# A two-layer attention and mixture block: the layer-0 mixing spread over three engines, with reordered stages

## The reference

```python
xn = _layernorm(x)
x = x + attention0(xn) + ffn0(xn)
# ffn0: x_norm = rms(xn); logits = x_norm @ W.T + base
#   H_res = sinkhorn(H_res_logits / 0.1, 50 iterations); H_res = (1 - g) * I + g * H_res
#   H_pre, H_post = softmax(...), softmax(...)
#   y = einsum('btnc,btn->btc', streams, H_pre) @ W_branch
#   out = einsum('btij,btjc->btic', H_res, streams) + einsum('btc,btn->btnc', y, H_post)
xn = _layernorm(x)
x = x + attention1(xn) + ffn1(xn)
# attention1: q = xn @ Wq.T; latent k, v = down, then up; 32 heads, 4 of them on one key head, causal
# ffn1: xf @ weight.T + sum over the top 2 of 8 experts of gate * (xf @ A) @ B / 16
```

## Time and profile before

| | us |
|---|---|
| median of 3 runs (2345.44 to 2351.66) | 2350.42 |
| the profiled execution: time | 2352.82 |
| its span, granted TensorE clock 0.984 | 2351.0 |
| stage B begins; first sum of its scaling; its last reciprocal; last operation | 85.8; 86.8; 192.1; 238.6 |
| stage C0: last down product ends; last block's staging copy | 299.1; 359.9 |
| first attention stage: first query product; first scores; end | 366.5; 381.3; 1293.2 |
| stage C1: first and last block's staging copy | 1360.2; 1420.8 |
| second attention stage: first query product; end | 1440.0; 2351.0 |

### The profile page before, as it was taken

One profiled execution on the slowest core, in us unless ns is written; L12 is line 12 of the kernel. 1 busy time (PEld: TensorE's weight loads), 2 busy tenths in 40 slices (PEclk: granted clock), 3 DMA queues, 4 the chain that ended last, 5 costly groups with the idle time before them and its releaser, 6 DMA issues. The chain is left out here.

```text
span 2351.0 us, 34663 instructions
## 1 busy us (share of the span) xinstructions
PE 2226.2 (95%) x11190; PEld 1810.6 (77%) x11190; DVE 1536.4 (65%) x3818; ACT 1070.2 (46%) x2279; POOL 1014.8 (43%) x1124
## 2 busy tenths in 40 slices
PE   6799897999999999999998888999999999999998
PEld 5554676888888888878786767888888888888886
DVE  6777565777677777756565564656566666666665
ACT  2456233545554444445444232545454544444444
POOL 5331713444445453676764011525344444434341
PEclk9999998999999999999999999999999999999999
DMA  9600564010101010111100464010101010101000
GB/s 349 207 0 10 213 234 156 10 63 9 63 9 63 14 58 27 45 47 42 44 28 6 173 245 157 28 48 24 62 9 62 9 62 9 62 9 62 27 32 32
DMA packets 74168, 165.26 MB, mean 70 GB/s; under 512 B 4721, under 2 KB 38897, under 8 KB 67442
## 3 DMA queue, kind: packets, MB, share of 16 engines
q1 hardware_dynamic: 73650, 162.95, 19.7%
q10 hardware_dynamic: 432, 1.32, 0.1%
HBM read 113.40 MB, written 72.61 MB: 79 GB/s over the span
## 5 line engine op out<-in xcount | busy, mean ns | idle before, releaser
L1852 DVE TENSOR_TENSOR pT<-psum,pT 128x512 fp32r<-128x512 f32 x576 | 387.1, 688 | 262.1 <-ACT pT L1900 259.8
L1752 POOL TENSOR_TENSOR probs_even<-probs_even,rinv 128x1024 f32<-128x1024 f32 (+2 forms) x192 | 241.0, 1255 | 553.9 <-DVE rinv L1843 553.9
L1900 ACT ACTIVATE pT<-psum 128x512 fp32r<-128x512 f32 x576 | 330.9, 596 | 317.8 <-PE psum L1961 317.7
L1838 DVE CUSTOM_DVE_ANT_0 psum<-psum,causal 128x256 f32<-128x256 f32 (+7 forms) x512 | 385.8, 766 | 37.3 <-PE psum L97 33.4
L1891 ACT ACTIVATE probs_even<-psum,nmax 128x1024 f32<-128x1024 f32 (+3 forms) x256 | 204.3, 798 | 247.2 <-DVE nmax L1838 243.4
L1752 POOL TENSOR_TENSOR probs_odd<-probs_odd,rinv 128x896 f32<-128x896 f32 (+2 forms) x192 | 198.9, 1043 | 257.5 <-DVE rinv L1843 257.3
L95 PE MATMUL psum<-keys,q 128*128 128x512 f32 (+3 forms) x768 | 265.7, 346 | 3.7 <-DVE q L1793 2.8
L97 PE MATMUL psum<-keys,q 128*128 128x512 f32 (+3 forms) x768 | 262.1, 341 | 0.0
L96 PE MATMUL psum<-keys,q 128*128 128x512 f32 (+3 forms) x768 | 262.0, 341 | 0.0
L95 PE MATMUL psum<-pT,vals 128*128 128x512 f32 x576 | 256.6, 445 | 4.3 <-DVE pT L1852 0.4
L1891 ACT ACTIVATE probs_odd<-psum,nmax 128x896 f32<-128x896 f32 (+3 forms) x256 | 176.4, 690 | 146.0 <-DVE nmax L1838 143.1
(11 more groups left out here) (304 smaller groups left out, 4423.5 us busy)
## 6 DMA issues: line engine op xcount, KB each, us to landing
k_parts<-kv_out SPq DMA_DIRECT2D x32, 512.0 KB, 4.7
wq<-wq_copy SPq DMA_DIRECT2D x16, 1024.0 KB, 4.8
v_parts<-kv_out SPq DMA_DIRECT2D x32, 512.0 KB, 3.6
wo<-wo_copy SPq DMA_DIRECT2D x16, 1024.0 KB, 4.8
keys<-k_parts SPq DMA_DIRECT2D x32, 512.0 KB, 4.5
vals<-v_parts SPq DMA_DIRECT2D x64, 256.0 KB, 3.1
acc<-in_x SPq DMA_DIRECT2D x4, 1024.0 KB, 12.0
xn_later<-xn SPq DMA_DIRECT2D x1, 2048.0 KB, 14.7
```

What stands on the lines that cost most here:

```text
L1752: pool.tensor_tensor(p, p, rinv[:, u, h:h + 1].to_broadcast([P, (TB - u) * P]), ALU.mult).then_inc(p_ok, 1)
L1838: dve.tensor_tensor_reduce(out=row, in0=row, in1=causal[:, S - n:S], scale=-1.0, scalar=-2 * MASKED, op0=ALU.add, op1=ALU.min, accum_out=n ...
L1852: dve.tensor_tensor(pT[:, n % PT_SLOTS, 1, :], bank[T_BANK + n % 2], f32(pT[:, n % PT_SLOTS, 0, :]), ALU.subtract).then_inc(t_lo, 1)
L1900: act.activation(pT[:, n % PT_SLOTS, 0, :], bank[T_BANK + n % 2], ACT.Copy).then_inc(t_hi, 1)
```

## The change

In layer0_project GpSimd adds the bias to six tiles instead of five. In layer0_mix: the recentring and the maxima of tiles 0 and 1 stand before half 0, and 68 halves run in one loop; maxima of later units stand five halves apart instead of four, 20 a unit; ScalarE makes a tile's shares right behind its exponential and rounds weights in unit 2 tile by tile; TensorE makes the next unit's first scores before the heads' outputs, and two of the four outputs before branch_in; of batch 0's tiles VectorE mixes 0 to 3, GpSimd 4 and 5, ScalarE with TensorE 6 and 7 (through eight slots of their own, four of ten products among the last unit's turns); the last unit's adds of heads follow VectorE's mixing. In layer1_inputs: the spill (or its load), the wait for the down products and the query weights' load stand before all stores; MAINS is 6 for both batches, and batch 0's last two products follow the blocks; GATE_EXP goes from 8 to 12; the stage no longer waits for the last stores, SyncE and GpSimd do so at the head of the attention. In layer1_attention the mixing steps of blocks 2, 5, 6 and 7 change.

```diff
-            add_bo(3)
-            add_bo(4)
+            for t in range(3, TB - 2):
+                add_bo(t)
...
-        FIRST_MAX, PER_UNIT = 3, 17
-        BY_ACT, SHARE_SLOTS = range(TB - 3, TB), UQ
+        FIRST_MAX, PER_UNIT, HALVES = 7, 20, 2 * SINKHORN_ITERS - EARLY_HALVES
+        BY_POOL, BY_ACT, SHARE_SLOTS = range(TB - 4, TB - 2), range(TB - 2, TB), 8
...
+            pool.wait_ge(mix_ok, 1)
+            steps = 0
+            for t in BY_POOL:
+                x = x1[:, t, :].rearrange("p (i c) -> p i c", i=NS)
+                for j in range(NS + 1):
+                    stream = xn[:, t, j * D:(j + 1) * D] if j < NS else y[:, t, :]
+                    weight = T[:, t, :, j] if j < NS else rw[:, t, 1, :]
...
+                    pool.tensor_tensor(products[:], stream.unsqueeze(1).to_broadcast([P, NS, D]),
+                                       weight.unsqueeze(2).to_broadcast([P, NS, D]), ALU.mult).then_inc(blended, 1)
+                    pool.wait_ge(blended, steps + 1)
+                    pool.tensor_tensor(x, x, products[:], ALU.add).then_inc(blended, 1)
+                    steps += 2
...
+            between = {0: [(weights, 0)], 1: [(maximum, 2)], 3: [(maximum, 3)], 4: [(gates, 0)], 5: [(later_head, 0)],
+                       6: [(invert, t) for t in range(UQ)]}
+            for t in range(UQ, NT):
+                at = FIRST_MAX + PER_UNIT * (t // UQ - 1) + 5 * (t % UQ)
+                between.setdefault(at, []).append((maximum, t))
+                between.setdefault(min(at + 7, HALVES - 1), []).append((invert, t))
+            for t in range(NT - UQ):
+                between.setdefault(FIRST_MAX + PER_UNIT * (t // UQ + 1) + (1, 1, 3, 4)[t % UQ], []).append((add_heads, t))
+
+            weights_max(0)
+            dve.wait_ge(logs_ok, 2)
+            after(dve.tensor_tensor(Z[:], Z[:], wide_rows(lrow[:]), ALU.add))
+            dve.tensor_tensor(Z[:], Z[:], wide_cols(lcol[:]), ALU.add).then_inc(z_ok, 1)
             for k in range(PARTS):
+                dve.memset(part_of(col, k), 1.0).then_inc(factor_ok[k], 1)
+            maximum(0)
+            maximum(1)
+            for half in range(HALVES):
...
-            for tiles in ((0, 1), (2, 3, 4)):
+            for tiles in ((0, 1), (2, 3)):
...
+            for t in range(NT - UQ, NT):
+                add_heads(t)
...
+                            if unit == UNITS and j % 2:
+                                product(j // 2)
...
-                        if t == 1:
-                            share(0)
-                        if t == 2:
+                        share(t)
+                        if t == UQ:
...
+                        if unit == 2:
+                            if qt == 0:
+                                act.wait_ge(m.ffn_in, 16 * 5)
+                            weight_high(wf_h[:, qt, :], wf_l[:, qt, :])
...
+                if unit + 1 < UNITS:
+                    scores(UQ * unit + UQ)
                 if unit:
                     pe.wait_ge(o_ok, unit)
...
+                    head_out(UQ * unit - UQ)
+                    head_out(UQ * unit - UQ + 1)
                 if unit < UNITS:
                     branch_in(unit)
+                if unit:
+                    head_out(UQ * unit - UQ + 2)
+                    head_out(UQ * unit - UQ + 3)
...
-        MAINS = TB if first else 6
+        MAINS = 6
         SUMS = [("main", t) for t in range(MAINS)]
+        if first:
+            SUMS += [("main", t) for t in range(MAINS, TB)]
...
+            if first:
+                sp.wait_ge(lr_ok, HALVES)
+                sp.dma_start(m.tmp_s, tmpT[:]).then_inc(spilled, 16)
+            sp.wait_ge(dn_mm, len(downs))
+            if first:
+                sp.wait_ge(parts_out, 16 * 12)
+            sp.dma_start(f32(m.wq[b][:, 1]), m.wq_s[0]).then_inc(m.wq_in[b], 16)
+            if not first:
+                sp.dma_start(tmpT_first[:], m.tmp_s).then_inc(tmp_in, 16)
             for w, (kind, i, n) in enumerate(ups):
...
-            for i in range(SLOTS):
-                sp.wait_ge(stored[i], 16 * len(range(i, len(ups), SLOTS)))
...
-            mixing_steps = {2: (1, 1, 2), 4: (1, 1, 2), 5: (1, 1, 2), 6: (1, 1, 1)}
+            mixing_steps = {2: (1, 1, 3), 4: (1, 1, 2), 5: (1, 1, 1), 7: (0, 0, 3)}
...
+            for i in range(KV_SLOTS):
+                sp.wait_ge(m.stored[b][i], 16 * (UPS // KV_SLOTS))
             for k in range(2):
                 load(keys[:, k, :], keys_of(0, k)).then_inc(k_in, 16)
...
+            for i in range(KV_SLOTS):
+                pool.wait_ge(m.stored[b][i], 16 * (UPS // KV_SLOTS))
             pool.memset(causal[:], 0.0).then_inc(causal_ok, 1)
```

More of the change, by code:

```diff
@@ L44 @@
 MASKED = -1e30
+KV_SLOTS, UPS = 4, 32
 class Shared:
@@ L638, in add_heads @@
                 dve.wait_ge(p_inv, t + 1)
-                dve.scalar_tensor_tensor(out=x1[:, t, :], in0=bank[7 - t % 2][:], scalar=rinv[:, t:t + 1], in1=x1[:, t, :],
+                dve.scalar_tensor_tensor(out=x1[:, t, :], in0=out_bank(t), scalar=rinv[:, t:t + 1], in1=x1[:, t, :],
                                          op0=ALU.mult, op1=ALU.add).then_inc(x1_ok, 1)
[L642 to L648, removed]
@@ L674, in _ @@
+            for k in range(PARTS):
+                dve.wait_ge(factor_ok[k], 1 + HALVES)
             ours = T[:, 0:TB]
@@ L805, in branch, with scores, head_out @@
                 last.then_inc(y_mm, 1)
+            def scores(t):
+                if t >= 2:
+                    pe.wait_ge(p_exp, t - 1)
+                for half in range(2):
+                    ks = slice(t // TB * S + 512 * half, t // TB * S + 512 * half + 512)
+                    last = pe.matmul(bank[2 + 2 * (t % 2) + half][:], m.q0[:, t * P:t * P + P], m.k0[:, ks], start=True, stop=True)
+                last.then_inc(s_mm, 1)
+            def head_out(t):
+                if t % UQ >= 2 and t < NT - UQ:
+                    pe.wait_ge(x1_ok, t - 1)
+                qs = slice(t % UQ * P, t % UQ * P + P)
+                pe.matmul(out_bank(t), oT[:, qs], wo0[:], start=True, stop=True).then_inc(wo_mm, 1)
             for unit in range(UNITS + 1):
-                b, bp = unit * UQ // TB, (unit - 1) * UQ // TB
+                bp = (unit - 1) * UQ // TB
                 for qt in range(UQ):
                     if unit < UNITS:
-                        t = UQ * unit + qt
-                        if t >= 2:
-                            pe.wait_ge(p_exp, t - 1)
-                        for half in range(2):
-                            ks = slice(b * S + 512 * half, b * S + 512 * half + 512)
-                            last = pe.matmul(bank[2 + 2 * (t % 2) + half][:], m.q0[:, t * P:t * P + P], m.k0[:, ks], start=True, stop=True)
-                        last.then_inc(s_mm, 1)
+                        if qt or not unit:
+                            scores(UQ * unit + qt)
                     if unit:
@@ L924, in layer1_inputs @@
         kv_mm, kv_hi, kv_lo = sem("kvmm"), sem("kvhi"), sem("kvlo")
-        stored = [sem(f"stored{i}") for i in range(SLOTS)]
+        stored = m.stored[b]
         spilled, tmp_in = sem("spilled"), sem("tmp_in")
@@ L1239, in _ @@
                 add_sum(added)
+                added += 1
                 low_rank_low(3)
-                for p in range(added + 1, TOTAL):
-                    add_sum(p)
+            for p in range(added, TOTAL):
+                add_sum(p)
         @block.scalar
```

155 lines of the change are left out of this document (65 added, 90 removed).

## The result

The changed kernel takes 2355.88 us (median), the kernel before 2350.51 beside it: the ratio is 1.0019 with an interval of 1.0012 to 1.0026. Instead of 17 us less it takes 4.5 us more by the ratio (5.4 by the medians), outside the range of 2315 to 2346. The profiled execution has a span of 2353.0 us against 2351.0 before.

What follows compares the result with a forecast made beforehand. It took TensorE-VectorE handovers to bound layer-0 mixing and TensorE the attention stages. Terms -2.4 (mixing), -11.8 and -2.0 (first inputs), -8 (second inputs), +7 (first attention) sum to -17.2: from 2350.4 to about 2333 us, range 2315 to 2346.

Steps and rivals of the forecast that it cites:

- Keys behind the wait ("+7"): First attention stage: keys queued behind a load that waits for mixing come late in iterations 5 and 6; net +7 us.
- Rival (4): First attention stage: late keys leave TensorE at its lower clock much longer; 2358 us and more; chance 0.05.
- C0 ("31 x 1.36 = 42.2 to 348.3"): First input stage: TensorE paces the key and value blocks at 1.36 us each; attention starts 11.8 us earlier.
- 0 here: First input stage: GpSimd's split delays VectorE about 3 us, but TensorE's six banks of lead make the cost 0.
- the clock: First input stage: TensorE's 10.86 us pause falls, and with it the granted clock of 0.50 behind it; -2.0 us.
- Rival (3): Input stages: stores stay the bound, four slots going round in 1.5 us a block; total near 2350 us; chance 0.08.
- C1 ("-8"): Second input stage: earlier stores bring the shares earlier, -7.0 us, and fewer slow multiplications, -1.0; together -8 us.
- Stage B ("-2.4"): Layer-0 mixing stage: scaling ends at 188.8 and the stage at 236.2 instead of 238.6; -2.4 us.
- The alternation of VectorE and GpSimd: Mixing in the layer-0 stage: VectorE gets one operation through per GpSimd operation, 20 in 26 us.
- Rivals (1): Layer-0 mixing: VectorE and GpSimd don't clash; that stage -18.6 us, the whole 2317; chance 0.17.
- (2): Layer-0 mixing: GpSimd keeps the port for all 24 us; that stage +7 us, the whole 2342; chance 0.08.
- (5): First attention stage: the keys aren't late, so +7 becomes -5; the whole 2321 us; chance 0.12.

Runs made afterwards that it cites:

- e2: The kernel before with only the new mixing steps of the first attention stage: 2369.69 us, ratio to the kernel before 1.0081.
- f2: The changed kernel with four more 0.5 MB spills among the blocks of the first input stage: 2360.13 us, ratio to the kernel before 1.005.
- f1: The changed kernel with GpSimd's split of the query weights behind the twelfth block in both input stages: 2349.9 us, ratio to the kernel before 0.9998.
- g1: The kernel before with only the new layer0_mix and the sixth bias add: 2354.84 us, ratio to the kernel before 1.0015.
- g2: The kernel before with the new layer0_mix, but tiles 4 and 5 mixed by VectorE instead of GpSimd: 2344.59 us, ratio 0.9968.
- h1: The kernel before with the new layer0_mix, but the first four maxima behind halves 0, 1, 3 and 4: 2353.23 us, ratio 1.0002.

## Why the prediction was wrong

By its own steps:

- **Keys behind the wait ("+7"): mechanism right, size wrong.** This is the step that failed most: the stage lost 19.4 us in the profile (16 between the means of all profiles, 19 in e2). Late keys were foreseen at both places, at 4 us of wait and 2 of clock. The waits were 6.10 and 5.56, with 2.5 and 2.3 behind them. I had the keys ready 4.9 us after their issue, as when they go alone; they took 7.4. I had overlooked that the wait holds back more than the keys: the values and the output weights then go at the same time, and the third tile's loads 0.9 us ahead. With block 3's late norms (forecast 3.6 and 2.7, measured 3.85 and 2.86) iteration 5 cost 13.4 instead of 8.3, iteration 6 8.1 instead of 5.3. The waits in blocks 5 and 6 did not vanish: 1.93 and 1.53 took the place of 2.61 and 2.78. Iteration 7 gave back 2.8, not 6.6.
- **Rival (4)** named this loss as the slow side, at 18 us for each iteration, by a long slow clock. That price was never paid. The time went over by the sum of the errors below and above, not by one mishap.
- **C0 ("31 x 1.36 = 42.2 to 348.3"): wrong.** The blocks took 49.5, since the bytes are the bound (f2) and the first stores were late (f1). The cost of GpSimd's split beside VectorE, which I had put at "0 here" because TensorE has six banks of lead, was 2.5 us: the cover I named protects TensorE, while the queue of stores was what ran empty. The first block was right to 1 us. The two products fell wholly under the stores, 3.3 us better than I had it, and the clock gave 0.8 instead of 2.0. Sum -7.9 for -13.8. Rival (3), which I had at 0.08, held in that the stores are the bound, but not in its mechanism (slots with a fixed landing time, which f2 rules out) nor in its price.
- **C1 ("-8")**: -7.0. The shares came 6.5 us earlier after the stage's start, forecast 7.
- **Stage B ("-2.4")**: -1.6 in the profile, by errors that cancel. The scaling ended 2.6 earlier than my 188.8, the turns resumed at 207.3 instead of 212; but from there to the end it took 29 us and not 24: the turns and products with v took 12.8 instead of 10 (granted clock 0.50 up to 213, behind the wait of 8.30), and I had left out the 3.7 us of the last unit's four outputs ahead of the mixing's products. Over many executions the part isn't a gain: +3.5 alone (g1, 0.2 to 6.8). Of that, 1.8 is the stage itself in g1's profile, whose scaling had the low clock; the rest is not explained. The alternation of VectorE and GpSimd was right (20 operations in 26 us; 23 in 25.2). I did not draw what it implied: that with no share for GpSimd the stage would be 7.7 to 10 us shorter.
- **Rivals (1), (2) and (5)** fall: VectorE's operations took 1.07 us each beside GpSimd and not 0.265, it got 23 of them through and not none, and the keys were late.

In the profiles the errors are +12.4 (attention), +5.9 (C0), +1.0 (C1) and +0.8 (B); a start 0.7 earlier and a second attention stage 0.3 shorter, not of the change, bring the sum of -17.2 to the +2.0 of the spans.

## What to carry to other kernels

Before work is moved to a later place on a side engine, list every wait in the transfer queue that names that work, and what stands behind each: here one reordered pair of lines gave back 17.7 us. Before work is lent to an idle GpSimd, look up how long VectorE's operations take beside it. Here those that read two operands in SBUF waited (0.265 us became 1.07 in the mean, 0.42 became 1.45), and so did a tensor_scalar from SBUF to SBUF, first beside GpSimd, then without it:

```profile
246.74 1.64 DVE L1089 TENSOR_SCALAR xn<-acc,mv,rstd 128x512 f32<-128x512 f32 x1
...
1311.89 0.54 DVE L1089 TENSOR_SCALAR xn<-acc,mv,rstd 128x512 f32<-128x512 f32 x1
```

Operations with an operand in PSUM didn't: the heads' adds took 0.74 beside GpSimd and 0.75 before. In a stage full of stores in which the next block waits for a free slot, read the transfer share ahead of the engines: at 1.0 the transfers set the pace.

## What was not expected of the hardware

The same code of stage B, with the same code ahead of it, begins in some kernels' profiles with TensorE at its lower clock level (eight score products in 5.37 us, not 3.67) and in others not. An order with slack hides that (153.5 us either way), a tighter one shows it (151.9 to 155.3). Each kernel has one profile, so how often one and the same program does either isn't known. Stores of 0.5 MB settle at 1.24 to 1.30 us each, but one in ten to twenty of them takes 1.2 to 1.9 us more; what these are was not looked into. C0's blocks also took 2 us longer in g1 and g2 (50.6 and 50.4) than in the kernel before, e2 and h1 (48.4, 48.5 and 49.0) with the same code of that stage; that stays open.
